# A vision tower in one kernel: the second norm's tokens transposed by DMA, and base products, gate and transform moved within the round

## What is computed

```
h = patches @ W
x = layernorm(h)
modulated = (x @ in_w + in_b) * (gelu(x @ mod_w1 + b1) @ mod_w2 + b2)
y = irfft(rfft(modulated) * rfft(kernel))            # along the tokens of an image
h = h + y @ out_w + out_b
x = layernorm(h)                                     # the second norm
gate = softmax(x @ router_W.T + router_b)            # best 2 of 6, rescaled to sum 1
h = h + x @ base_W.T + base_b + shared + sum_e gate_e * (x @ A_e.T) @ B_e.T
```

## Time and profile before

| | |
|---|---|
| median of 3 runs | 1259.88 us (1257.22 to 1260.01) |
| profiled execution | 1259.47 us |
| its span, first to last instruction | 1257.7 us |
| TensorE busy | 97% |
| VectorE, ScalarE, GpSimd busy | 69%, 52%, 31% |
| mean granted TensorE clock | 0.999 |

### The profile page before, as it was taken

One profiled execution on the slowest core, in us unless ns is written; L12 is line 12 of the kernel. 1 busy time (PEld: TensorE's weight loads), 2 busy tenths in 40 slices (PEclk: granted clock), 3 DMA queues, 4 the chain that ended last, 5 costly groups with the idle time before them and its releaser, 6 DMA issues.

```text
span 1257.7 us, 20842 instructions
## 1 busy us (share of the span) xinstructions
PE 1221.5 (97%) x7906; PEld 1168.7 (93%) x7906; DVE 871.4 (69%) x2592; ACT 649.2 (52%) x1200; POOL 393.3 (31%) x459
## 2 busy tenths in 40 slices
PE   8999999999999999999999999999999999999998
PEld 8899999999999999999999999999999999999986
DVE  5567766667766667766677666677666677666776
ACT  6655455545555545555455555455555455554441
POOL 3523233232233232333232333322332322332220
PEclk9999999999999999999999999999999999999999
DMA  7310222120321211221202222202222112211001
GB/s 242 93 55 20 62 68 68 55 43 38 68 68 55 68 30 51 68 67 55 68 20 62 68 68 55 45 36 68 68 57 65 30 52 68 67 55 33 22 21 34
DMA packets 87201, 73.50 MB, mean 58 GB/s; under 512 B 66887, under 2 KB 81070, under 8 KB 83262
## 3 DMA queue, kind: packets, MB, share of 16 engines
q1 hardware_dynamic: 87102, 72.18, 20.3%
HBM read 43.07 MB, written 12.85 MB: 44 GB/s over the span
## 4 chain that ended last, share of the span: by engine, by line
PE 71%; DVE 15%; ACT 8%; issue 3%; DMA 2%; SPq 1%; POOL 0%; DVEq 0%
PE rotating L1460 11%; PE rotating L1462 11%; PE rotating L1461 11%; PE rows_ps L1460 10%; PE rows_ps L1461 9%; PE rows_ps L1462 9%; PE turn L1738 4%; DVE fold_l L1129 3%; ACT gelu L655 3%; ACT fold_h L678 2%; PE turn L1510 2%; DMA prod<-spec_y 2%; PE rows_ps L1520 1%; DVE spec_y L1136 1%; DVE prod L1137 1%
## 5 line engine op out<-in xcount | busy, mean ns | idle before, releaser
L655 ACT ACTIVATE gelu<-rotating,consts 128x392 f32<-128x392 f32 x256 | 142.5, 587 | 187.5 <-PE rotating L1462 187.5
L528 POOL TENSOR_TENSOR folded<-modulated 128x196 f32<-128x196 f32 x63 | 38.0, 603 | 546.1 <-DVE modulated L1119 546.1
L515 POOL TENSOR_TENSOR gelu_l<-gelu,gelu_h 128x784 fp32r<-128x784 f32 x62 | 115.6, 1883 | 255.6 <-DVE norm L1102 252.0
L510 POOL TENSOR_TENSOR patches_l<-patches,patches_h 128x384 fp32r<-128x384 f32 (+1 forms) x186 | 181.6, 1005 | 2.8 <-ACT patches_h L607 2.8
L1460 PE MATMUL rotating<-x_h,w_h 128*128 128x392 f32 x512 | 177.2, 346 | 1.6 <-ACT gelu L655 1.6
L1460 PE MATMUL rotating<-gelu_h,w_h 128*128 128x392 f32 x512 | 177.4, 347 | 0.0
L1462 PE MATMUL rotating<-x_h,w_l 128*128 128x392 f32 x512 | 174.7, 341 | 0.0
L1461 PE MATMUL rotating<-x_l,w_h 128*128 128x392 f32 x512 | 174.5, 341 | 0.0
L1461 PE MATMUL rotating<-gelu_l,w_h 128*128 128x392 f32 x512 | 174.2, 340 | 0.0
L1462 PE MATMUL rotating<-gelu_h,w_l 128*128 128x392 f32 x512 | 174.0, 340 | 0.0
L1460 PE MATMUL rows_ps<-tokw_h,patches_h 128*128 128x256 f32 x570 | 163.1, 286 | 1.6 <-DVE patches_l L872 1.6
(11 more groups left out here) (296 smaller groups left out, 2922.0 us busy)
## 6 DMA issues: line engine op xcount, KB each, us to landing
patches<-dram_x_rest SPq DMA_DIRECT2D x30, 1152.0 KB, 5.1
out<-h_sb SPq DMA_DIRECT2D x30, 384.0 KB, 2.5
prod<-spec_y SPq DMA_TRANSPOSE x62, 3.2
patches<-dram_x_first SPq DMA_DIRECT2D x2, 384.0 KB, 5.9
h_sb<-dram_x_second SPq DMA_DIRECT2D x1, 768.0 KB, 7.6
patches<-dram_x_fourth SPq DMA_DIRECT2D x1, 768.0 KB, 9.3
h_sb<-dram_first SPq DMA_DIRECT2D x2, 320.0 KB, 3.1
gelu<-dram_w SPq DMA_DIRECT2D x1, 512.0 KB, 8.2
```

Source lines behind the costliest of these rows:

```text
L510: pool.tensor_tensor(patches_l[:, k, 0:n], patches[:, k, 0:n], patches_h[:, k, 0:n].bitcast(F32), ALU.subtract).then_inc(pool_patches_lo, 1)
L515: pool.tensor_tensor(gelu_l[:, 2 * j:2 * j + 2, :], gelu[:, 2 * j:2 * j + 2, :], gelu_h[:, 2 * j:2 * j + 2, :].bitcast(F32), ALU.subtract)\
L528: pool.tensor_tensor(folded[:, m, 0, :, 1:NF], fwd, back, ALU.add)
L655: act.activation(gelu[:, k, :], bank(g + 1, UP[k])[:, 0:GT], ACT.Gelu, bias=b1_bias[:, k:k + 1]).then_inc(act_gelu, 1)
```

## The change

- **The second norm is transposed by DMA.** `turn_x2` goes. VectorE writes the low and the high halves of `norm2` apart into `spec_y` (`part_tokens`, behind `modulate(mid, 0)`); SyncE issues one DMA transpose of 12 blocks from `spec_y` to `prod` (`transpose_x2`, at the end of its round); VectorE joins the halves in `norm2` (`join_x2`, behind `modulate(mid, 1)`). `x2_hi` now reads `norm2` in SBUF and stands in the next round behind `fold_halves(back, 1)`; `x2_lo` reads SBUF too and stands behind `join_x2`. Since `spec_y` and `prod` are shared with the fold, `fold_halves` waits for the tokens' transpose to land, and the fold's transposes wait for `join_x2`.
- **The gate runs without interruption**: `cosine_whole` before it, `fold_lo` behind it.
- **`base_route` stands behind `mlp_up` 1**, not ahead of `mlp_up` 0; **`turn_gated` behind `mlp_up` 6** (the seventh), not 5; **`dft` behind `routed`**; `inverse_dft` behind two embedded tiles, not one.
- On VectorE `gelu_lo` 2 and `finish` stand ahead of the products of the spectrum. On ScalarE `sine_whole`, `fold_hi` and `gelu_hi` shift by a tile.
- For the last group but one the fold is transposed on TensorE (`turn_fold`, eight transposes) and not by DMA.

The diff, cut to its core:

```diff
             def transpose_fold(g):
                 for m in range(DH):
                     sp.wait_ge(act_halves, DH * g + m + 1)
-                    if g > 0 and m == 0:
-                        sp.wait_ge(dve_y, DH * g)
+                    if m == 0:
+                        if g > 0:
+                            sp.wait_ge(dve_y, DH * g)
+                            sp.wait_ge(dve_x2_whole, g)
                     sp.dma_start_transpose(turned_rows[:, :, m, :], half_rows[:, m]).then_inc(fold_turned, 16)
+
+            def transpose_x2(d):
+                sp.wait_ge(dve_token_halves, 2 * d + 2)
+                sp.dma_start_transpose(x2_turned_rows, token_halves).then_inc(x2_turned, 16)
...
                 act.wait_ge(pool_fold, DH * g + m + 1)
                 if g > 0 and m == 0:
                     act.wait_ge(pe_idft, DH * g)
+                    act.wait_ge(x2_turned, 16 * g)
...
-            def x2_hi(d, ps, hi):
-                n = len(output_tiles(d)) * TILE
+            def x2_hi(d):
+                act.wait_ge(dve_x2_whole, d + 1)
                 for m in range(DH):
-                    act.wait_ge(pe_turn_x2, DH * d + m + 1)
-                    act.activation(hi[:, m, 0:n], ps[:, m, 0:n], ACT.Copy).then_inc(act_x2_hi, 1)
+                    act.activation(x2_h[:, m, :], x2_whole[:, m, :], ACT.Copy).then_inc(act_x2_hi, 1)
...
                     fold_halves(back, 0)
                     project(mid, (0,))
                     fold_halves(back, 1)
+                    if in_range(tail):
+                        x2_hi(tail)
                     project(mid, (1,))
...
+            def part_tokens(d):
+
+                dve.wait_ge(dve_norm2, d + 1)
+                for b in range(2):
+                    dve.tensor_copy(token_parts[:, b], norm_parts[:, b]).then_inc(dve_token_halves, 1)
+
+            def join_x2(d):
+                dve.wait_ge(x2_turned, 16 * (d + 1))
+                dve.tensor_copy(x2_whole_halves, x2_turned_halves).then_inc(dve_x2_whole, 1)
+
+            def x2_lo(d):
                 for m in range(DH):
                     dve.wait_ge(act_x2_hi, DH * d + m + 1)
-                    dve.tensor_tensor(lo[:, m, 0:n], ps[:, m, 0:n], hi[:, m, 0:n].bitcast(F32), ALU.subtract)\
+                    dve.tensor_tensor(x2_l[:, m, :], x2_whole[:, m, :], x2_h[:, m, :].bitcast(F32), ALU.subtract)\
...
-                if in_range(tail):
-                    base_route(tail, rows_ps, x2_h, x2_l)
                 if in_range(mid - 1):
                     pe.wait_ge(dve_mod, DH * mid)
                 mlp_up(mid, 0)
                 pe.wait_ge(act_in, DH * mid + 1)
                 mlp_up(mid, 1)
+                if in_range(tail):
+                    base_route(tail, rows_ps, x2_h, x2_l)
...
-                if in_range(back):
-                    dft(back)
                 pe.wait_ge(act_gelu, HC * mid + 3)
                 mlp_up(mid, 5)
                 pe.wait_ge(act_gelu, HC * mid + 4)
+                mlp_up(mid, 6)
+                pe.wait_ge(act_gelu, HC * mid + 5)
                 if in_range(tail):
                     turn_gated(tail, bank(i, TURN_GATED))
-                pe.wait_ge(act_gelu, HC * mid + 5)
-                mlp_up(mid, 6)
+                pe.wait_ge(act_gelu, HC * mid + 6)
+                mlp_up(mid, 7)
                 if in_range(tail):
                     routed(tail, rows_ps)
-                pe.wait_ge(act_gelu, HC * mid + 6)
-                mlp_up(mid, 7)
+                if in_range(back):
+                    dft(back)
```

More of the change, by code:

```diff
@@ L1128, in fold_lo @@
                 dve.wait_ge(act_fold_hi, g + 1)
-                dve.tensor_tensor(fold_l[:, :, :], whole[0:NF, :, :], fold_h[:, :, :].bitcast(F32),
+                rows = turn if g == GROUPS - 2 else whole
+                dve.tensor_tensor(fold_l[:, :, :], rows[0:NF, :, :], fold_h[:, :, :].bitcast(F32),
                                   ALU.subtract).then_inc(dve_fold_lo, 1)
@@ L1372, in _ @@
                 if in_range(back):
+                    real_products(back)
+                    imaginary_products(back)
                     spectrum_of_y(back)
-                for j in range(0 if i == 1 else 2, 4):
-                    gelu_lo(mid, j)
+                gelu_lo(mid, 3)
                 if in_range(back):
@@ L1401, in _ @@
                 if in_range(back):
-                    x2_lo(back, rows_ps, x2_h, x2_l)
+                    join_x2(back)
+                    x2_lo(back)
             last = GROUPS - 1
+            fold_lo(last - 1)
             gate_range(last - 2, round_routes, round_room)
-            cosine_whole(last - 1)
             gate_exp(last - 2, round_room)
-            fold_lo(last - 1)
             gate(GATE_STEPS * (last - 2) + EXP_STEPS, round_routes, round_room)
@@ L1723, in keep_clock, with turn_fold @@
                     pe.matmul(ps[:, 0:BANK], row[:, 0:P], row, start=True, stop=True)
+            def turn_fold(g):
+                pe.wait_ge(pool_fold, DH * g + 2)
+                for x in range(2):
+                    for img in range(PAIR):
+                        for m in range(DH):
+                            c = img * DIM + m * P
+                            ins = pe.transpose(turn[0:NFP, x, c:c + P], folded[:, m, x, img, :], ident[:, :])
+                ins.then_inc(pe_turn_fold, 1)
             def dft(g):
@@ L1847, in _ @@
                 mlp_down(mid, 1, range(turn_at, HC))
-                if in_range(back):
-                    turn_x2(back, rows_ps, norm2)
             last = GROUPS - 1
             project(last)
-            base_route(last - 2, rows_ps, x2_h, x2_l)
+            turn_fold(last - 1)
             pe.wait_ge(dve_mod, DH * last)
```

98 lines of the change are left out of this document (50 added, 48 removed).

## The result

The changed kernel takes 1345.57 us (median of four runs, 1344.79 to 1345.86) against 1259.09 us for the kernel before on the same chip: 6.9% slower, ratio 1.0688 with an interval of 1.0669 to 1.0706. The forecast was 1334 us, its range 1282 to 1372. The profiled execution took 1344.79 us, span 1343.0.

The account below looks back on a forecast made before the run. TensorE, busy for 97% of the span, was taken to bound the kernel. Four waits on 36.55 us gave 40.65 us a round against 38.12; over 29 rounds +74 us on 1259.5, so 1334 us, range 1282 to 1372.

Parts of the forecast that it names:

- The sum: Whole round: 36.55 us left without transposes and old waits, plus 0.5, 2.2, 0.9 and 0.5, makes 40.65 us.
- Part 1: Project, at T, its start: the six transposes leave TensorE, but their 0.58 us returns as a wait of 0.5 us.
- Part 2: Tokens' road from norm to base products: these start at T + 6.6 (T: project's start), a wait of 2.2 us.
- The landing: End of the tokens' 12-block DMA transpose: 4.2 us after issue, bounds 3.2 and 4.8, so at T + 2.1.
- ScalarE's chain: Fold copies, project and token copies queued behind the landing, then the second subtraction: base products can start 3.5 us after it.
- GpSimd's part: At the token subtractions, VectorE waits for GpSimd's patch instructions: 1.0 us, between bounds of 0 and 2.0.
- Rival (b): Tokens land at or under T + 0.9: no wait for base products, 38.45 us a round, 1269 us; chance 0.08.
- Rival (a): GpSimd does not get in VectorE's way: base wait of 0.8 us, 39.25 us a round, 1292 us; chance 0.22.
- Rival (c): Faster: tokens land early, gate and y_lo keep up, TensorE bound by its own work; 36.55 us a round, 1214; chance 0.06.
- Rival (d): Everything collides: landing at T + 2.8, GpSimd's full 2 us; 42.35 us a round, 1382 us; chance 0.14.
- Part 3: Gate before the turn: 5.9 us of VectorE steps, a turn wait of 0.9 us; the wait for the fold is gone.
- Part 4: Mixer: y_lo ends 4.3 us after the inverse transform starts, TensorE has 3.9 us of work: a wait of 0.5 us.

Follow-up runs that it names:

- e1_tokens_on_tensore: The changed kernel with the second norm's tokens transposed by TensorE again (six transposes, no DMA road), all else as changed: 1269.23 us.
- e8_small_patches: The changed kernel with GpSimd's subtractions of patches 2 to 7 cut to 8 columns from the sixth round on: 1295.11 us.
- e3_filled_wait: The changed kernel with eight extra matmuls that nothing reads put into TensorE's wait ahead of the base products: 1328.46 us.
- e12_base_behind_one: e1_tokens_on_tensore with three down products ahead of the mixer, base products behind one up block, ScalarE's fold work ahead of its second GELU: 1238.85 us.
- e7_turn_behind_eight: e1_tokens_on_tensore with the turn behind all eight up blocks, transform next, then routed products, first half of down products behind the last GELU: 1275.18 us.
- e2_gpsimd_waits: The changed kernel with GpSimd's last four patch subtractions of a round held back until VectorE has subtracted the tokens: 1308.54 us.

## Why the prediction was right

**The sum.** 40.65 us a round forecast, 40.93 measured over the 29 steady rounds; against 38.16 before, that is 80.3 of the 85.3 us between the two profiled executions, and the rest lies at the ends. (40.65 is 2.53 more than 38.12 and not 2.55, which is 0.6 us in the forecast.) Within those 40.93, the clock gives 0.47 and the rest 40.46. The four waits as measured add up to 36.55 + 0.52 + 1.95 + 0.87 + 0.39 = 40.28. The missing 0.18 is a cost that the sum had for the mixer alone: behind a wait the second matmul is late as well, 0.27 us behind the first in place of 0.16 at the base products, 0.20 in place of 0.12 at the mixer. So the mechanism was right, wait by wait, and the closeness of the time is in part luck: without the clock, which I had not foreseen, it would have been 1328 to 1332 us.

**Part 1, project: right.** 0.5 forecast, 0.44 to 0.59 measured, in the place of the six transposes' 0.58: taking them off TensorE gained next to nothing.

**Part 2, base products: the place right (T + 6.33 against T + 6.6), by luck, since two errors cancel.** The landing: I took 4.2 us for 12 blocks and half a microsecond for a collision of the part copies with GpSimd. The transpose took 3.7 us, and in that collision GpSimd waited, not VectorE; with project itself 0.2 us later than I had it, the tokens landed at T + 0.95 and not T + 2.1. The term mis-sized by choice was the 4.2, near the middle of my bounds of 3.2 and 4.8; the trace shows 3.2 for 8 blocks and 3.7 for 12. The Trainium skill's effective 261 GB/s (DMA: Bandwidth & Descriptors, Latency and other measured facts) had given an estimated 0.5 us for the larger transfer, and the trace agrees. ScalarE's chain from there to the base products, forecast at 3.5, took 3.57 (token copies done at 662.85, 0.55 for an undisturbed second subtraction, less the 0.40 of the late fold copy and the landing at 659.43). GpSimd's part, forecast at 1.0 between bounds of 0 and 2.0, took 1.75, close to the upper bound: 1.35 at the token subtractions (done at 664.75 instead of 663.40) and 0.40 through the fold copy that the joining copy had held up. That second path runs through GpSimd, which I had let hold VectorE up but not be held up itself with ScalarE waiting for it. The wait came out at 1.95 against 2.2.

**Rival (b)** set a landing at or under T + 0.9 as its condition, and that was all but met. What it drew from it, no base wait, was wrong: the 3.5 us behind the landing reach to T + 4.45, where TensorE has just arrived, and GpSimd's 1.75 come on top. Its time, 1269 us, is that of e1_tokens_on_tensore, where the road is away altogether. **Rival (a)**, GpSimd not in the way, comes nearest to e8_small_patches, 1295.1 us against its 1292, and did not happen by itself. **Rival (c)** needed a gate of under 5.4 us; without interruption it took 5.89 (median), its steps no shorter than before. **Rival (d)** needed the landing at T + 2.8.

**Part 3, gate: right.** 0.9 forecast, 0.83 to 0.91 measured, and again 0.83 (median) in e1_tokens_on_tensore, so it doesn't depend on the tokens. The wait for fold_l went, as said.

**Part 4, mixer: right.** 0.5 forecast, 0.29 to 0.46 measured.

**The missing term, the clock.** The prediction lists what a wait costs in microseconds of idle time. Nine rounds in 29 paid 1.5 us more, 13.6 us in all; with the three falls outside them it is up to the 17.1 of e3_filled_wait.

## What to carry to other kernels

A wait on the bound engine is covered one for one by any of its work that is ready and that nobody waits for; move such work (here three down products, 15 us), and before moving other work ask what it is covering now. Start a serial chain on another engine earlier rather than put its consumer later: with e12_base_behind_one three quarters of the wait vanished, with e7_turn_behind_eight all of it came back behind the turn. Before an operand is moved from PSUM to SBUF, look at what GpSimd does in that stretch, and at whatever runs in the stretch to which you then push GpSimd.

## What was unexpected of the hardware

- TensorE's granted clock fell to 0.50 (1.2 GHz) for about 3.5 us behind a wait of 1.9 us that was in every round, but only in every third round, 123 us apart. With base waits of 0.7 us (e8_small_patches, e2_gpsimd_waits) it falls in none of the 29 rounds, not even behind the turn's wait of 1.45 us in e2_gpsimd_waits; their mean clock is 0.997, against 0.985 for the changed kernel. What decides in which round it falls, no run here shows.
- A two-column copy of GpSimd can last 1.01 us and an 18-column step of VectorE 0.79 us, four to five times their own time, because the other engine was first. Which of the two waits changed with the order in time and not with the size of either.
- A DMA transpose of 8 blocks lands in 3.2 us and one of 12 in 3.7, so most of it doesn't depend on the size; single ones of 8 blocks took up to 4.9 (e7_turn_behind_eight).
